# A decoder layer's attention steps: the division of a pair's output goes behind the second block maximum, and the turn of the row maxima goes one fifth of a step later

## The reference, cut to what matters

```python
x = x + attn(layernorm(x))    # 32 query heads, 16 key heads, head size 32, causal, 512 keys
x = x + xattn(layernorm(x))   # 32 query heads, 8 key heads, 64 context rows, a mask is added
x = x + ffn(layernorm(x))     # silu(x Wg^T) * (x Wu^T), then Wd^T; 3584 hidden, NF4 codes
# attn: w = softmax(where(causal, q k^T * scale, -inf)); out = w v
```

## Time and profile before

| | |
|---|---|
| median of 3 runs | 2859.84 us (2858.97 to 2860.97) |
| the profiled execution, its own time | 2857.48 us |
| its span, first to last instruction | 2855.5 us |
| mean granted TensorE clock | 0.958 |

### The profile page before, as it was taken

One profiled execution on the slowest core, in us unless ns is written; L12 is line 12 of the kernel. 1 busy time (PEld: TensorE's weight loads), 2 busy tenths in 40 slices (PEclk: granted clock), 3 DMA queues, 4 the chain that ended last, 5 costly groups with the idle time before them and its releaser, 6 DMA issues.

```text
span 2855.5 us, 52508 instructions
## 1 busy us (share of the span) xinstructions
PE 2603.0 (91%) x18464; PEld 1395.8 (49%) x18464; DVE 2070.3 (73%) x2844; ACT 1572.5 (55%) x2794; POOL 1233.5 (43%) x1068
## 2 busy tenths in 40 slices
PE   5989989889986518899999999999999999999999
PEld 3656666666665414344444444444444444444444
DVE  6556667567676657987868778787887878788773
ACT  3456555556565257664747456474655647465550
POOL 2356566566577323433425243342434324243340
PEclk9999999989998759999999999999999999999999
DMA  5342433332231150211112111121211111121112
GB/s 188 92 140 88 118 108 94 96 112 68 82 101 62 34 180 24 66 52 45 59 42 69 37 52 52 44 60 43 66 37 56 54 44 60 37 66 37 59 33 118
DMA packets 153267, 205.32 MB, mean 72 GB/s; under 512 B 34160, under 2 KB 85872, under 8 KB 153072
## 3 DMA queue, kind: packets, MB, share of 16 engines
q1 hardware_dynamic: 153072, 202.97, 22.8%
HBM read 157.16 MB, written 44.04 MB: 70 GB/s over the span
## 4 chain that ended last, share of the span: by engine, by line
PE 59%; DVE 2%; issue 1%; ACT 1%; DMA 1%; POOL 0%; SPq 0%; DVEq 0%; ACTq 0%; POOLq 0%
PE f_bank L1487 39%; PE f_down L1507 20%; DVE line L1611 1%; DMA codes<-in_codes 1%; DVE f_stats L1625 0%; DVE fT_l L1638 0%; ACT f_xn L1547 0%; ACT line L1536 0%; ACT fT_h L1555 0%; PE f_down L1469 0%; DVE w L1617 0%; ACT line L1533 0%; DVE h L1647 0%; DVE y L1652 0%; DVE f_mean_var L1628 0%
## 5 line engine op out<-in xcount | busy, mean ns | idle before, releaser
L1611 DVE TENSOR_TENSOR line<-line 128x512 f32<-128x512 f32 x1008 | 924.0, 967 | 44.4 <-issue 29.4
L1536 ACT ACTIVATE line<-codes 128x512 f32<-128x512 int32 x1008 | 591.2, 620 | 383.6 <-DVE line L1611 285.5
L1487 PE MATMUL f_bank<-fT_h,up_h 128*128 128x512 f16 x1792 | 680.2, 380 | 3.7 <-DVE fT_l L1638 2.4
L1487 PE MATMUL f_bank<-fT_l,up_h 128*128 128x512 f16 x1792 | 680.2, 380 | 0.0
L1487 PE MATMUL f_bank<-fT_h,up_l 128*128 128x512 f16 x1792 | 680.2, 380 | 0.0
L537 POOL TENSOR_TENSOR p_l<-p,p_h 128x512 f16<-128x512 f32 x320 | 372.0, 1171 | 304.1 <-ACT p_h L941 303.6
L1652 DVE SCALAR_TENSOR_TENSOR y<-f_down,y 128x1024 f32<-128x1024 f32 x224 | 274.4, 1225 | 190.5 <-PE f_down L1507 190.5
L1101 DVE TENSOR_REDUCE block_max<-bank 128x4 f32<-128x512 f32 x320 | 218.6, 686 | 220.2 <-PE bank L696 218.0
L933 ACT ACTIVATE p<-bank 128x512 f32<-128x512 f32 x320 | 191.1, 597 | 332.1 <-PE bank L725 329.8
L1417 POOL TENSOR_TENSOR up_l<-w,up_h 128x512 f16<-128x512 f32 x112 | 145.2, 1297 | 526.2 <-ACT up_h L1541 526.2
L1412 POOL TENSOR_TENSOR w<-w,scales 128x512 f32<-128x512 f32 x168 | 263.9, 1571 | 229.0 <-DVE w L1617 229.0
(11 more groups left out here) (153 smaller groups left out, 4247.8 us busy)
## 6 DMA issues: line engine op xcount, KB each, us to landing
codes<-in_codes SPq DMA_DIRECT2D x168, 256.0 KB, 3.0
scales<-in_scales SPq DMA_DIRECT2D x336, 128.0 KB, 2.9
nat_parts<-nat SPq DMA_DIRECT2D x48, 256.0 KB, 2.0
q_rows<-nat_parts SPq DMA_DIRECT2D x96, 128.0 KB, 3.1
x_unit<-in_x SPq DMA_DIRECT2D x64, 128.0 KB, 2.7
x<-x_unit SPq DMA_DIRECT2D x64, 128.0 KB, 2.4
y<-x SPq DMA_DIRECT2D x4, 2048.0 KB, 11.8
out<-y SPq DMA_DIRECT2D x16, 512.0 KB, 2.6
```

Source lines behind the costliest of these rows:

```text
L1487: mm = nc.tensor.matmul(bank[(GATE, UP)[kind] + n % 2][:, :], w[:, chunk, kind, P * c:P * c + P], x[:, c, cols], start=(m == 0), stop=(m = ...
L1536: op = nc.scalar.activation(line[:, m, :], codes[:, slot, :], ACT.Copy, scale=slope, bias=intercept)
L1611: nc.vector.tensor_tensor(line[:, n + 2, :], line[:, n, :], line[:, n + 2, :], ALU.max)\
```

## The change

Three moves, nothing added or removed. VectorE calls pair_out(s-2) in fifth 1, behind maximum(s+2, 1), instead of in fifth 0 behind maximum(s+2, 0) and ahead of x_soft. In even steps TensorE calls turn_max in fifth 2, behind that fifth's score and t_score, instead of in fifth 1. ScalarE calls max_rows in fifth 2 likewise, behind that fifth's exponential. SP's order stays.

```diff
@@ TensorE, step @@
+                    if k == 2 and s % 2 == 0 and 0 <= s < NS:
+                        turn_max(s // 2)
                     if k == 1:
-                        if s % 2 == 0 and 0 <= s < NS:
-                            turn_max(s // 2)
                         if y is not None:
@@ ScalarE, step @@
-                    if k == 1 and s % 2 == 0 and 0 <= s < NS:
+                    if k == 2 and s % 2 == 0 and 0 <= s < NS:
                         max_rows(s // 2)
@@ VectorE, step @@
                     if 0 <= s + 2 < NS:
                         maximum(s + 2, k)
+                    if k == 1 and 2 <= s <= NS + 1:
+                        pair_out(s - 2)
                     if k == 0:
-                        if 2 <= s <= NS + 1:
-                            pair_out(s - 2)
                         if x is not None:
```

## The result

| | before | after |
|---|---|---|
| median | 2859.62 us (2858.97 to 2864.9, 6 runs) | 2873.31 us (2866.8 to 2875.43, 6 runs) |
| profiled execution, own time and span | 2857.48, 2855.5 | 2873.79, 2871.9 |
| mean granted clock | 0.958 | 0.957 |

The ratio is 1.0042, 95% interval 1.0029 to 1.0055: 12 us slower (8 to 16). The forecast was 25.7 us. The direction and the range (2868 to 2901) held, the sum did not.

A forecast was written before the change was run, and what follows sets the result against it. TensorE, busy 91%, was taken to bound the kernel, so VectorE's order counts only where TensorE waits. Copies 15.9 + last steps 9.1 + SP queue 3.2 - gains 2.5 = +25.7 us, giving 2885.5 us, range 2868 to 2901.

The forecast's parts named there:

- Gains of both parts: Negation out of nat's way 0.9 us plus earlier v bias 1.6 us: 2.5 us gained, bounds 0 and 5.
- (b): Nearly all other steps up to 56: VectorE has slack ahead of what follows, so the later division costs zero.
- Part one: Row maxima turned and negated in fifth 2 of even steps: copy waits cost 15.9 us, 0.9 us given back.
- part two: Division behind the second block maximum: 9.1 us in steps 57 to 65, queue 3.2 us, v bias gain 1.6 us.
- Copy waits: TensorE's fifth-3 score in 16 even steps waits for the late copy of maxima into q_rows: +15.9 us.
- Negation: ScalarE's negation no longer delays the nat part in fifth 1: 0.15 us in each of six steps, 0.9 us gained.
- v bias: Steps 5, 21 and 37: the bias no longer stands behind the division, for which TensorE waited; 1.6 us gained.
- Steps 57 to 65: Late division holds GpSimd's pair addition and low parts, with no projection to cover it: +9.1 us, from 0 to 13.5.
- The load in steps 26 and 42: Later pair store on SP's queue delays the next batch's row load: 1.6 us each, 3.2 in all, bounds 0 and 5.
- Only part one costs: Rival: GpSimd and SP have slack, so only the late copies cost: +13.4 us, 2873; chance 0.13.
- The clock rival: Rival: TensorE's clock falls behind some 16 new waits, about 1.5 us lost each: +24 more, 2910; chance 0.12.

The follow-up runs named there:

- e2: Kernel before with only turn_max and max_rows moved to fifth 2, the division left in fifth 0: 2872.10 us, ratio 1.0044.
- e3: Kernel before with only the division moved behind block maximum 1, the turn left in fifth 1: 2890.72 us, ratio 1.0106.
- e8: Kernel before, with GpSimd's second low part of a step waiting, from step 20 on, for VectorE's nat part of fifth 0: 2844.84 us, ratio 0.9946.
- e7: Changed kernel with GpSimd's add_pair moved behind low_part(5s-3): 2879.54 us, ratio 1.0065.
- e9: Changed kernel with the same GpSimd wait for the nat part as in e8, from step 20 on: 2875.14 us, ratio 1.0046.
- e5: Kernel before, unchanged, run again for a second profile: 2859.69 us, span 2857.7.
- e1: Changed kernel, unchanged, run again for a second profile: 2869.32 us, ratio 1.0035.

## Why the forecast was wrong by half

**The step that failed** is the last term of the sum, "Gains of both parts: 0.9 + 1.6 = 2.5; bounds 0 and 5", and behind it two sentences: that the negation out of nat's way is worth its own 0.15 us in six steps, and, under (b), that where VectorE has slack ahead of what follows a later division is worth zero. The place was the right one: the forecast saw that px_l ends TensorE's wait, that VectorE runs without a gap from nat to px_l, and that both moves act there. It took nat's 1.23 us as the length of that instruction, and that was two lengths: 0.69 of work and 0.55 behind GpSimd. The changed kernel starts nat 0.15 us earlier (the negation's move) and, because GpSimd's addition waits for the late division, the low part later, and so the order of the two turned over. Neither move did it in all places alone: e2 left 43 of 45 nat parts at 1.23 us, e3 about half of them.

Sized by the runs, the order is worth 15.4 us (e8), where the whole term was 2.5 with 5 as its bound. Two other ways lead to less, and to far more than nothing. Part one alone measured +12.4 (e2) against the 15.0 that the forecast has for it; part two on top of it was forecast at 9.1 + 3.2 - 1.6 = 10.7 and measured 12.0 - 12.4 = -0.4, so that about 11 us are missing, and it is with part two that the order turned over. In e7, which puts the old order back, the same account gives about 10: 6.6 us slower than the changed kernel by their ratios, though the last steps got 6.7 back for 3.3 in the loads. What the forecast did count, 25.7, is what e9 against e8 shows, 28.6, or 25.9 by their profiled executions, and 25.7 less 10 to 15 is 11 to 16, where 12.0 was measured.

**Point by point.** *Copy waits, +15.9:* right in cause and nearly all places, a little too large; in 15 of the 16 places named they add to 13.6 us (step 18 by its growth), in step 30 px_l came last in this profile, and e2 has +12.4 with part of the gain in it. Not foreseen were step 4 (+1.1), steps 18 and 19, +3.1 together in the first profile against 0.6, and the waits behind the late division in steps 60 and 62. In steps 40, 44, 48 and 56 e9 minus e8 has 1.0 against 0.8 in the forecast; after minus before showed only 0.4, since nat's order gave the rest back. *Negation, 0.15 a step:* right to the hundredth. The wait in step 38 is 1.90 before, 1.36 in e8 and 1.20 in e9 and after: 0.54 for the order, 0.16 for the negation. *v bias, 1.6:* right in the wait, but mostly not in the time. Step 5 was 0.57 us shorter, and in steps 21 and 37 the wait of the earlier trace rows went from 1.35 to 0.77. But there px_l came later, and TensorE's wait for it rose from 0.24 to 0.91 and from nothing to 0.91: step 21 was 0.1 us longer. The waits for px_l in steps 25, 41 and 57 rose too (1.77 to 2.01, and 1.29 to 2.01 twice). That is part two's, since e3 has these waits and e2 hasn't, and under (b) the forecast had put it at zero. Step 20 was 0.53 shorter at another wait, that for kx_l (L761, 1.17 to 0.64). Step 37, TensorE after:
```profile
569.41 0.63 PE L639 MATMUL bank<-ident,xn 128*128 128x128 f32 x4 [0.77 <-DVE proj L1089]
...
574.55 0.39 PE L723 MATMUL bank<-q_rows,k_rows 97*128 97x512 f16 x1 [0.91 <-DVE px_l L1140]
```
*Steps 57 to 65, +9.1:* right as a sum and a little small. From step 57 to the last product of the cross part it took 95.2 us before and 106.2 after, 95.7 and 106.6 in e5 and e1, and 95.7 and 106.2 in e8 and e9: +10.5 to +11.0 (the +8.0 of the table has 2.4 us less behind this point, outside the change). The waits for o came at the addition (121.5 us in 63 places for 9.0 in 6) and at TensorE's turn in three steps. The single steps were not as forecast: by e9 and e8 step 58 grew by 0.1 and not 1.35, step 60 by 3.7 and not 1.0. *The load in steps 26 and 42, 1.6 each above the copy's 1.2:* these steps grew by 2.3 and 2.2 us, 1.8 each by e9 and e8; the forecast had 2.8.

**The rivals.** "Only part one costs" gives 2873, which is the time measured, but it isn't what happened: steps 57 to 65 cost some 11 us, and e9 against e8 has the full sum. A forecast that hit the number this way would have been right by accident. The clock rival, 2910, is out as a forecast of the time, and so is its condition, that each new wait brings a slow stretch: from 80 us to step 19, with nine new waits, the granted clock was at the lower level for 17.1 and 20.5 us in the two profiles of before and for 20.5 in both of the changed kernel. Between steps 19 and 39 it was there for 37.5 and 23.9 us in the two profiles of before, and for 10.2 and 13.7 in those of the changed kernel. But in the last steps it had something right: from step 57 to the last product of the cross part the lower level lasted 39.5, 39.2 and 38.9 us before, in e5 and in e8, and 65.2, 65.6 and 65.2 after, in e1 and in e9. How much of the 11 us there is the clock's isn't separated. The wait of 4.07 us that went away was charged twice in its way, as a wait and in the slow stretch behind it.

**What stays open.** How much of the 15 us between steps 19 and 39 is nat itself and how much the clock isn't separated everywhere: 5.0 us are steps 34 and 35, 3.7 the five steps with the px_l wait (0.40 to 0.94 each), both of which follow nat; 6.1 are steps 25, 29, 37 and 39, which were short in e5 too; and 2.2 are step 36, which had 3.4 us at the lower clock before, in e5 and in e8 and none after, in e1, e2 and e9. Since e2 has nat at 1.23 us and e8 at 0.69, that stretch does not follow nat, and what it follows isn't known. So 8.7 us in this stretch are shown to follow nat, 0.7 of them by the negation; the load in step 26 took 2.3 of it all back. Why the store of step 33 lands later when issued later isn't known.

## What to carry to other kernels

Before a duration goes into a sum, compare it with the same shape elsewhere in the trace: a minimum of 0.68 and a median of 1.23 us for one instruction say that it mostly waits inside itself, and the engine it waits for is found by laying its row beside the other engine's. A move on one engine must then be followed to who starts first on the other, for a tenth of a microsecond can turn 0.55 us over at every place. Where such a pair is found, set its order with a wait and measure that by itself: here it brought 0.5%. The two moves that happened to cause it cost more than that.

## What the runs showed of the hardware

- VectorE and GpSimd, each reading two SBUF tiles of 128x512: alone 0.69 and 1.16 us; GpSimd first, VectorE's takes 1.23 (started 0.48 later), 1.59 (0.11 later) or 1.69 (0.01 later); VectorE first by 0.10 or 0.04, GpSimd's takes 1.62 or 1.67. The later one ends 0.55 (VectorE's) or 1.02 us (GpSimd's) behind the first, in all 438 places of 12 profiles.
- The store of nat in step 33, issued 0.55 us later relative to its step, landed in 3.2 to 4.1 instead of 2.0 to 2.3 us: 6 profiled executions with the one and 6 with the other, and none between.
- Behind TensorE's wait of 4.07 us the granted clock was 0.50, behind one of 1.58 in the same place it stayed at 1.00.
- Two executions of the same kernel differed by 2.2 us (before) and 8.4 us (changed) in their spans, partly in stretches of 3.4 us at the lower clock; steps 25, 29 and 39 were 1.6 to 1.7 us longer in the one profile of the kernel before that had one there.
